# Causal attention in one kernel: the products that only serve the row maxima run as pairs of 64-row matmuls, the result gets a second bank, and the rotary sum moves to VectorE

## The chip, the core and the metric

The kernel runs on one core of a Trainium2 chip. Its engines are TensorE (PE in the rows, with its weight loads as PEld), VectorE (DVE), ScalarE (ACT), GpSimd (POOL) and SyncE (SP), which issues the transfers. The metric is the device time of one execution in microseconds (us). TensorE's results land in PSUM, which has eight banks of 512 fp32 columns; GpSimd has no access to PSUM.

## The reference

One transformer layer over 2048 tokens of width 512: a layer norm, attention with 32 query heads in 8 groups (4 query heads share one key head and one value head, all of width 64), and a feed-forward part with ternary weights. What matters here is the attention of one group:

```python
y = x * rsqrt(mean(x * x) + eps) * rms_w
q, k, v = split(y @ w_in.T)              # per group: 4 heads of q, one k, one v, width 64
q, k = rope(q), rope(k)                  # [x1*cos - x2*sin, x2*cos + x1*sin]
qk = (q @ k.T) * 64 ** -0.5              # causal: key <= query
attn = softmax(where(causal, qk, -inf))
o = attn @ v
```

## The kernel before

Everything fp32 is carried as two fp16 numbers, a high and a low part. After the norm (`normalise`), the function `attention` runs the eight groups one after another; then follow the output projection and the feed-forward part, which the change leaves alone.

In a group there are 16 **units** (4 chunks of 512 queries by 4 heads, `u = 4c + h`), and a unit of chunk c has 4(c+1) **steps**, one for each tile of 128 keys: 160 steps in a group. A step i goes through the engines so:

- `scores(i)` on TensorE: keys by queries, two products of 128 rows (high parts against `k_hl`, the low parts and the row maximum through `q_lm` and `k_h1`), and on the diagonal a third that adds the mask. The step is 512 columns wide, on the diagonal 512, 384, 256 and 128.
- `exps(i)` on ScalarE (L670) writes p in fp32; `low_part(i)` on GpSimd (L817) makes its low part.
- `values(i)` on TensorE, 5 steps later (`PV_LAG`): for each of up to four query tiles three matmuls of 64 or 65 columns (L619, L621, L623), which add up in the result bank `obank`.
- After the last step of a unit, `unit_out` on VectorE divides by the row sums (L776, L778); then ScalarE and GpSimd split the result in two parts (`unit_high`, `unit_low`).

The softmax needs each query's maximum **before** its scores are used. It comes from **pieces**: `max_piece` (L587) multiplies one tile of 128 queries with up to 512 keys, and VectorE reduces the bank (`reduce_piece`, L740, and L744 on the diagonal). There are 160 pieces in a group as well. The stationary tile is `q_hh`, which holds the high part of q twice, on rows 0 to 63 and on rows 64 to 127; `k_hl` holds the key's low part on rows 0 to 63 and its high part on rows 64 to 127, and `k_h1` holds the high part on rows 0 to 63. So a piece is (high q)(low k + high k). Any number near the true maximum serves, since it cancels out in the softmax.

Beside that, TensorE projects the coming tiles of 128 tokens (`project`, 12 matmuls of 384 columns, 16 tiles in a group). VectorE takes each out of its bank (`out_of_bank`): L763 and L769 for v, L765 and L766 for the products with cos and sin. GpSimd adds these (`rope_sum`, L823), and ScalarE and GpSimd split the sum (`qk_high_part`, `qk_low_part`).

The order on each engine is written out by hand: `SLOTS` has one slot for each step, with the projection and the pieces that ride in it. The pieces of a chunk are spread over a range of slots (`PIECE_SLOTS`), one or two in a slot. In a slot TensorE issues scores, the first piece, values, the projection, further pieces; where a unit begins, values come last. Pieces and projections share the **side banks** in turn (`take_bank`): with `SIDE = 4` an item waits until the reader of the item four places before it is done. The banks are 3 for scores, 4 at the side, and 1 for the result.

## Time and profile before

| | |
|---|---|
| median of 3 runs | 2151.24 us (2150.31 to 2152.04) |
| time of the profiled execution | 2150.29 us |
| its span, first to last instruction | 2148.2 us |
| attention, first to last step on GpSimd | 106.2 to about 1588 us |
| one group of eight (group 3) | 186.4 us, from 672.4 to 858.8 us |
| busy in that group: PE / POOL / DVE / ACT | 175.7 / 176.3 / 124.2 / 102.4 us |

Busy times are unions of an engine's instructions in a window. Matmuls are pipelined: a 512-column matmul is shown with 0.38 us, and the next starts 0.22 us after it. So the distance of the starts tells how much of TensorE a matmul takes, and a busy time of PE is a little too long at each place where it stops.

### The profile page before, as it was taken

The numbers are of one execution on the slowest core, as the hardware profiler recorded it, in microseconds if no ns is written. First come the engines' busy times: TensorE is split into PE (matmuls) and PEld (weight loads), VectorE is DVE, ScalarE is ACT, GpSimd is POOL, SyncE is SP. The second block draws the span as 40 slices with busy tenths as digits, with TensorE's granted clock in tenths as the row PEclk, the third lists the DMA queues.
The fourth block names the chain that finished last, engine by engine and source line by source line (L and its number), as shares of the span: only waits on it lengthen the run. The fifth ranks groups of instructions, "written<-read, shape, count | busy, mean of one in ns | idle before, by whom it ended". The sixth has DMA issues, their size and how long they took to land. (4 is left out here: it accounts for less than half of the span.)

```text
span 2148.2 us, 55361 instructions
## 1 busy us (share of the span) xinstructions
PE 1948.1 (91%) x21382; PEld 1178.0 (55%) x21382; DVE 1249.7 (58%) x3158; ACT 931.8 (43%) x1985; POOL 1587.4 (74%) x1803
## 2 busy tenths in 40 slices
PE   2599999999999999999999999999969988999998
PEld 1256666666666666666666666666634443444443
DVE  8567657757765764776576477657724772221221
ACT  3245555555555555555555555555541111111110
POOL 5489999999999999999999999999952441221311
PEclk7699999999999999999999999999989999999999
DMA  5432133124223312322332232223136530000000
GB/s 178 124 70 51 41 71 67 43 44 82 48 41 71 75 38 54 71 46 46 69 72 41 51 70 46 46 56 74 36 103 213 196 124 14 5 15 20 0 20 20
DMA packets 301573, 137.05 MB, mean 64 GB/s; under 512 B 248208, under 2 KB 285328, under 8 KB 299792
## 3 DMA queue, kind: packets, MB, share of 16 engines
q1 hardware_dynamic: 301328, 133.69, 26.4%
q8 instruction: 166, 2.72, 0.5%
q14 instruction: 79, 0.65, 0.1%
HBM read 49.74 MB, written 25.17 MB: 35 GB/s over the span
## 5 line engine op out<-in xcount | busy, mean ns | idle before, releaser
L817 POOL TENSOR_TENSOR pl<-p 128x512 f16<-128x512 f32 (+3 forms) x1280 | 1140.7, 919 | 89.0 <-ACT p L670 88.0
L670 ACT ACTIVATE p<-a_ps 128x512 f32<-128x512 f32 (+3 forms) x1280 | 676.3, 532 | 671.2 <-PE a_ps L603 430.5
L740 DVE TENSOR_REDUCE mpart<-a_ps 128x1 f32<-128x512 f32 x768 | 518.7, 687 | 169.4 <-PE a_ps L587 162.7
L619 PE MATMUL a_ps<-v,p 128*128 128x65 f16 x4352 | 528.5, 193 | 83.7 <-DVE onorm L778 60.7
L619 PEld LDWEIGHTS a_ps<-v,p 128*128 128x128 bf16 x4352 | 410.6, 97 | 218.9 <-DVE onorm L778 97.8
L621 PE MATMUL a_ps<-v,p 128*128 128x64 f16 x4352 | 530.1, 194 | 0.0
L623 PE MATMUL a_ps<-v,pl 128*128 128x65 f16 x4352 | 526.9, 192 | 0.0
L621 PEld LDWEIGHTS a_ps<-v,p 128*128 128x128 bf16 x4352 | 405.9, 97 | 98.4
L587 PE MATMUL a_ps<-k_hl,q_hh 128*128 128x512 f16 (+3 forms) x1280 | 439.8, 349 | 18.9 <-issue 11.4
L603 PE MATMUL a_ps<-q_lm,k_h 128*128 128x512 f16 (+3 forms) x1280 | 444.8, 347 | 0.0
L602 PE MATMUL a_ps<-q_hh,k_hl 128*128 128x512 f16 (+3 forms) x1280 | 444.1, 347 | 0.0
L623 PEld LDWEIGHTS a_ps<-v,pl 128*128 128x128 f16 x4352 | 407.2, 99 | 0.0
L744 DVE CUSTOM_DVE_ANT_0 masked<-a_ps,causal 128x128 bf16<-128x128 f32 (+3 forms) x512 | 247.9, 485 | 114.9 <-PE a_ps L587 107.9
L1264 POOL TENSOR_TENSOR f_hl<-f_hid,f_hh 128x512 f16<-128x512 f32 x64 | 74.2, 1161 | 239.9 <-DVE f_hh L1234 239.9
L1179 PE MATMUL f_ps<-xh,tern 128*128 (+1 forms) x512 | 195.0, 381 | 1.8 <-DVE f_credit L1221 1.8
L587 PEld LDWEIGHTS a_ps<-k_hl,q_hh 128*128 128x128 f16 x1280 | 124.0, 98 | 132.0 <-issue 14.0
L1179 PE MATMUL f_ps<-xl,tern 128*128 (+1 forms) x512 | 194.9, 381 | 0.0
L574 PE MATMUL a_ps<-wh,yh 128*128 128x384 f16 x512 | 168.8, 330 | 7.9 <-DVE wl L730 7.9
L984 PE MATMUL p_ps<-p_wh,p_att 128*128 128x512 f16 x512 | 158.6, 386 | 15.1 <-DMA p_att<-attn_scratch 15.1
L574 PE MATMUL a_ps<-wl,yh 128*128 128x384 f16 x512 | 168.8, 330 | 0.0
L574 PE MATMUL a_ps<-wh,yl 128*128 128x384 f16 x512 | 168.6, 329 | 0.0
L1215 ACT ACTIVATE f_silu<-f_ps,tern_scale 128x512 f32<-128x512 f32 x64 | 44.0, 687 | 256.7 <-PE f_ps L1179 256.7
(97 smaller groups left out, 2432.9 us busy)
## 6 DMA issues: line engine op xcount, KB each, us to landing
attn_scratch<-o_turn SPq DMA_DIRECT2D x64, 256.0 KB, 2.8
p_att<-attn_scratch SPq DMA_DIRECT2D x32, 512.0 KB, 4.5
raw<-ffn_t SPq DMA_DIRECT2D x12, 1024.0 KB, 5.0
wraw<-w_in_t SPq DMA_DIRECT2D x8, 768.0 KB, 5.2
resid_scratch<-xin SPq DMA_DIRECT2D x4, 1024.0 KB, 4.3
raw<-w_out_t SPq DMA_DIRECT2D x1, 4096.0 KB, 14.6
x<-resid_scratch SPq DMA_DIRECT2D x4, 1024.0 KB, 8.0
out<-x SPq DMA_DIRECT2D x16, 256.0 KB, 2.0
```

The lines of the kernel that those rows point to most:

```text
L574: last = nc.tensor.matmul(bank[:, 0:GC], a[:, kt, tok], b[:, kt, :], start=(kt == 0 and n == 0), stop=(kt == KT - 1 and n == 2))
L587: nc.tensor.matmul(bank[:, 0:width], q_hh[:, c % 2, h, t * P:(t + 1) * P], k_hl[:, par ^ ahead, kk * CHUNK:kk * CHUNK + width], start=True ...
L602: nc.tensor.matmul(out, k_hl[:, side, keys], q_hh[:, c % 2, h, r * P:CHUNK], start=True, stop=False)
L603: last = nc.tensor.matmul(out, k_h1[:, side, keys], q_lm[:, c % 2, h, r * P:CHUNK], start=False, stop=not diag)
L619: nc.tensor.matmul(o, weights, v[:, par, j, 0:VU], start=(j == 0 and t == 0), stop=False, skip_group_check=True)
L621: nc.tensor.matmul(o[:, 0:DH], weights, v[:, par, j, VL:VW], start=False, stop=False, skip_group_check=True)
L623: last = nc.tensor.matmul(o, pl[:, i % RING, t * P:(t + 1) * P], v[:, par, j, 0:VU], start=False, stop=(j == TPC * c + t), skip_group_chec ...
L670: nc.scalar.activation(p32[:, i % RING, r * P:CHUNK], sbank(i)[:, r * P:CHUNK], ACT.Exp, scale=SCALE).then_inc(exp_done, 1)
L740: nc.vector.reduce_max(mpart[:, u % 2, t, kk:kk + 1], bank, AX.X).then_inc(maxs_used, 1)
L744: nc.vector.tensor_tensor_reduce(masked[:, n % 2, 0:width], bank, causal[:, CHUNK - width:CHUNK], 1.0, -LEAST, ALU.add, ALU.max, mpart[:, ...
L817: nc.gpsimd.tensor_tensor(pl[:, i % RING, cols], p32[:, i % RING, cols], p_high[:, i % RING, cols], ALU.subtract).then_inc(low_ready, 1)
L1179: last = nc.tensor.matmul(bank, w[:, k, e * P:(e + 1) * P], x[:, k, bass.ds(c * CHUNK, CHUNK)], start=(k == 0 and x is xh), stop=(k == KT ...
```

## The change

Three things change in `attention`.

- **Pieces in pairs.** Two pieces that follow each other are issued together (`max_pair`). The first reads rows 0 to 63 of `q_hh` and of `k_h1`, the second rows 64 to 127 of `q_hh` and of `k_hl`; each contracts 64 rows and is (high q)(high k) alone. They go to two side banks. The slots are the same, but a slot has two pieces or none, and all pieces stand ahead of the slot's values and projection. The opening is arranged the same way.
- **Two result banks.** `OBANKS = 2`, so that the values of a unit wait for the unit before the last one to leave. For this `SIDE` goes from 4 to 3. `unit_out`, `unit_high` and `unit_low` come one step later.
- **The rotary sum on VectorE.** `out_of_bank` writes the sin product to a small `rope_b` (2 tiles instead of 4), the cos product back to its place in the bank, and the sum of the two to `rope_a`. GpSimd's `rope_sum` is gone. A side bank with a projection is now free after the sum (`roped_ready`), where it was free after L769 (`v_low`).

```diff
-SIDE = 4
-HIGH_LAG = PV_LAG + 1
-LOW_OUT_LAG = PV_LAG + 2
+SIDE = 3
+OBANKS = 2
+HIGH_LAG = PV_LAG + 2
+LOW_OUT_LAG = PV_LAG + 3
...
-        for n, piece in enumerate(chunk):
-            pieces[begin + n * (end - begin) // len(chunk)].append(piece)
+        for n in range(0, len(chunk), 2):
+            pieces[begin + n * (end - begin) // len(chunk)] += chunk[n:n + 2]
...
-        rope_b = sb("rope_b", [P, TILES_KEPT, HG + 1, DH], F32)
+        rope_b = sb("rope_b", [P, 2, HG + 1, DH], F32)
...
-        obank = ps[:, SBANKS + SIDE, 0:TPC * VU]
+        obank = lambda u: ps[:, SBANKS + SIDE + u % OBANKS, 0:TPC * VU]
...
-                        pe.wait_ge(v_low, (g + ahead) * TT + arg[0] + 1)
+                        pe.wait_ge(roped_ready, (g + ahead) * TT + arg[0] + 1)
...
-                def max_piece(ahead, u, i):
+                def max_pair(pair):
+                    ahead, u, i = pair[0]
                     c, h = divmod(u, HG)
-                    t, kk = divmod(i, c + 1)
...
-                    bank = take_bank("piece", ahead, u, i)
-                    width = CHUNK if kk < c else (t + 1) * P
-                    nc.tensor.matmul(bank[:, 0:width], q_hh[:, c % 2, h, t * P:(t + 1) * P],
-                                     k_hl[:, par ^ ahead, kk * CHUNK:kk * CHUNK + width], start=True, stop=True)\
-                        .then_inc(maxs_ready, 1)
+                    banks = [take_bank("piece", *piece) for piece in pair]
+                    for (_, _, i), bank, keys, rows in zip(pair, banks, (k_h1, k_hl), (slice(0, DH), slice(DH, P))):
+                        t, kk = divmod(i, c + 1)
+                        width = CHUNK if kk < c else (t + 1) * P
+                        nc.tensor.matmul(bank[:, 0:width], q_hh[rows, c % 2, h, t * P:(t + 1) * P],
+                                         keys[rows, par ^ ahead, kk * CHUNK:kk * CHUNK + width], start=True, stop=True)\
+                            .then_inc(maxs_ready, 1)
...
-                    if j == 0 and g + u:
-                        pe.wait_ge(o_out, g * UNITS + u)
+                    if j == 0 and g * UNITS + u >= OBANKS:
+                        pe.wait_ge(o_out, g * UNITS + u + 1 - OBANKS)
...
-                    for piece in pieces[:1]:
-                        max_piece(*piece)
+                    for n in range(0, len(pieces), 2):
+                        max_pair(pieces[n:n + 2])
...
-                    dve.wait_ge(qk_low, gg * TT + t + 1)
                     nc.vector.tensor_scalar(v[:, side, t, 0:DH], bank[:, ROPED:GC], 1.0 / W_SCALE, None,
                                             ALU.mult).then_inc(v_high, 1)
-                    nc.vector.tensor_tensor(roped(rope_a), halves, by_half(cos[:, t, :]), ALU.mult)
-                    nc.vector.tensor_tensor(roped(rope_b), halves[:, :, ::-1, :], by_half(sin[:, t, :]), ALU.mult)\
+                    if gg * TT + t >= 2:
+                        dve.wait_ge(roped_ready, gg * TT + t - 1)
+                    nc.vector.tensor_tensor(by_head(rope_b[:, t % 2]), halves[:, :, ::-1, :], by_half(sin[:, t, :]), ALU.mult)\
                         .then_inc(rope_parts, 1)
+                    dve.wait_ge(rope_parts, 2 * (gg * TT + t) + 1)
+                    nc.vector.tensor_tensor(halves, halves, by_half(cos[:, t, :]), ALU.mult).then_inc(rope_parts, 1)
                     dve.wait_ge(v_high, gg * TT + t + 1)
                     nc.vector.scalar_tensor_tensor(v[:, side, t, VL:VW], bank[:, ROPED:GC], 1.0 / W_SCALE,
-                                                   v[:, side, t, 0:DH], ALU.mult, ALU.subtract).then_inc(v_low, 1)
+                                                   v[:, side, t, 0:DH], ALU.mult, ALU.subtract)
+                    dve.wait_ge(rope_parts, 2 * (gg * TT + t) + 2)
+                    dve.wait_ge(qk_low, gg * TT + t + 1)
+                    nc.vector.tensor_tensor(by_head(rope_a[:, b]), halves, by_head(rope_b[:, t % 2]), ALU.add)\
+                        .then_inc(roped_ready, 1)
...
-                    if step is not None and step - PV_LAG + 1 in FIRST_STEP[1:]:
-                        unit_out(FIRST_STEP.index(step - PV_LAG + 1) - 1)
+                    if step is not None and step - PV_LAG in FIRST_STEP[1:]:
+                        unit_out(FIRST_STEP.index(step - PV_LAG) - 1)
...
-                def rope_sum(ahead, t):
-                    b = t % TILES_KEPT
-                    pool.wait_ge(rope_parts, (g + ahead) * TT + t + 1)
-                    nc.gpsimd.tensor_tensor(rope_a[:, b], rope_a[:, b], rope_b[:, b], ALU.add).then_inc(roped_ready, 1)
```

On TensorE, at slots 9 to 11 of the first group (unit 1 begins in its values), before the change. L602 and L603 are scores, L587 pieces, L619, L621 and L623 values; names in brackets are the semaphores waited for.

```order
L602 MATMUL a_ps<-q_hh,k_hl 128x512 [waits exp_done]
L603 MATMUL a_ps<-q_lm,k_h 128x512
L587 MATMUL a_ps<-k_hl,q_hh 128x128 [waits maxs_used]
L619 MATMUL a_ps<-v,p 128x65 [waits low_ready,exp_done,o_out]
...
L602 MATMUL a_ps<-q_hh,k_hl 128x512 [waits exp_done]
L603 MATMUL a_ps<-q_lm,k_h 128x512
L587 MATMUL a_ps<-k_hl,q_hh 128x512 [waits maxs_used]
L619 MATMUL a_ps<-v,p 128x65 [waits low_ready,exp_done]
...
L602 MATMUL a_ps<-q_hh,k_hl 128x512 [waits exp_done]
L603 MATMUL a_ps<-q_lm,k_h 128x512
L587 MATMUL a_ps<-k_hl,q_hh 128x256 [waits maxs_used]
L619 MATMUL a_ps<-v,p 128x65 [waits low_ready,exp_done]
```

The same place after it; L603 and L604 are scores now, L588 the pieces, L620, L622 and L624 values.

```order
L603 MATMUL a_ps<-q_hh,k_hl 128x512 [waits exp_done]
L604 MATMUL a_ps<-q_lm,k_h 128x512
L620 MATMUL a_ps<-v,p 128x65 [waits low_ready,exp_done,o_out]
...
L603 MATMUL a_ps<-q_hh,k_hl 128x512 [waits exp_done]
L604 MATMUL a_ps<-q_lm,k_h 128x512
L588 MATMUL a_ps<-k_h,q_hh 128x512 [waits maxs_used]
L588 MATMUL a_ps<-k_hl,q_hh 128x256
L620 MATMUL a_ps<-v,p 128x65 [waits low_ready,exp_done]
...
L603 MATMUL a_ps<-q_hh,k_hl 128x512 [waits exp_done]
L604 MATMUL a_ps<-q_lm,k_h 128x512
L620 MATMUL a_ps<-v,p 128x65 [waits low_ready,exp_done]
```

The piece of slot 9 has gone to slot 8, that of slot 11 to slot 10, and the two of slot 10 read `k_h` and `k_hl`; between a pair and the next stand products of 128 rows. The first values of the unit still name `o_out`, but with a smaller value.

On VectorE, where unit 0 leaves its bank and a tile is taken out in the same slot, before:

```order
L776 RECIPROCAL rden<-a_ps 128x4 [waits pv_done]
L778 TENSOR_TENSOR onorm<-a_ps,rden 128x256 [waits o_rden]
L763 TENSOR_SCALAR v<-a_ps 128x64 [waits qk_low,misc_ready]
L765 TENSOR_TENSOR rope_a<-a_ps,cos_sb 128x320
L766 TENSOR_TENSOR rope_b<-a_ps,sin_sb 128x320
L769 SCALAR_TENSOR_TENSOR v<-a_ps,v 128x64 [waits v_high]
L744 ISA masked,mpart<-a_ps,causal 128x128 [waits maxs_used,maxs_ready]
```

The same after:

```order
L761 TENSOR_SCALAR v<-a_ps 128x64 [waits misc_ready]
L765 TENSOR_TENSOR rope_b<-a_ps,sin_sb 128x320 [waits roped_ready]
L768 TENSOR_TENSOR a_ps<-a_ps,cos_sb 128x320 [waits rope_parts]
L770 SCALAR_TENSOR_TENSOR v<-a_ps,v 128x64 [waits v_high]
L774 TENSOR_TENSOR rope_a<-a_ps,rope_b 128x320 [waits qk_low,rope_parts]
L781 RECIPROCAL rden<-a_ps 128x4 [waits pv_done]
L783 TENSOR_TENSOR onorm<-a_ps,rden 128x256 [waits o_rden]
```

The tile's part has a fifth instruction, the sum, and a wait between the two products; the unit's part (L776 and L778 before, L781 and L783 after) has moved behind the tile's, one slot later.

On GpSimd, in the same stretch (L817 low parts of p, L823 the rotary sum, L832 low parts of q and key, L840 the low part of a result), before:

```order
L840 TENSOR_TENSOR o_hl<-onorm,o_hl 128x4x64 [waits o_high]
L817 TENSOR_TENSOR pl<-p 128x512 [waits exp_done] x2
L823 TENSOR_TENSOR rope_a<-rope_a,rope_b 128x320 [waits rope_parts]
L832 TENSOR_TENSOR qk_lo<-rope_a,qk_hi 128x5x64 [waits qk_high]
L817 TENSOR_TENSOR pl<-p 128x512 [waits exp_done] x2
L840 TENSOR_TENSOR o_hl<-onorm,o_hl 128x4x64 [waits o_high]
```

And after (L820, L830, L838):

```order
L838 TENSOR_TENSOR o_hl<-onorm,o_hl 128x4x64 [waits o_high]
L820 TENSOR_TENSOR pl<-p 128x512 [waits exp_done]
L830 TENSOR_TENSOR qk_lo<-rope_a,qk_hi 128x5x64 [waits qk_high]
L820 TENSOR_TENSOR pl<-p 128x512 [waits exp_done] x3
L838 TENSOR_TENSOR o_hl<-onorm,o_hl 128x4x64 [waits o_high]
```

The sum is gone from the queue, and the result's low part comes one step later.

## Rows read from the trace of the kernel before

**Rows 1.** The page: its first line and its row of PE.

```profile
span 2148.2 us, 55361 instructions
...
PE 1948.1 (91%) x21382; PEld 1178.0 (55%) x21382; DVE 1249.7 (58%) x3158; ACT 931.8 (43%) x1985; POOL 1587.4 (74%) x1803
```

**Rows 2.** Busy time by stage of group 3, stages cut at L817 starts.

```profile
core 0: us, PE busy (x) PEld busy (x) DVE busy (x) ACT busy (x) POOL busy (x), PEclk, DMA share, GB/s
672.40:691.40 19.00, 18.92 (x210) 12.61 (x207) 14.77 (x48) 10.21 (x28) 16.76 (x25) 1.00 0.36 78
691.40:709.00 17.60, 16.20 (x244) 10.98 (x243) 13.08 (x38) 11.07 (x24) 17.59 (x23) 1.00 0.35 69
709.00:728.90 19.90, 18.85 (x226) 12.13 (x225) 13.70 (x40) 9.09 (x23) 18.79 (x25) 1.00 0.24 54
728.90:755.80 26.90, 25.66 (x364) 17.02 (x363) 22.99 (x56) 16.80 (x37) 26.32 (x30) 1.00 0.39 71
755.80:783.90 28.10, 25.74 (x354) 16.93 (x352) 18.70 (x45) 14.74 (x32) 25.86 (x31) 1.00 0.10 21
783.90:807.90 24.00, 22.82 (x291) 14.27 (x287) 16.66 (x42) 13.47 (x28) 22.54 (x27) 1.00 0.36 67
807.90:823.20 15.30, 14.83 (x226) 9.96 (x226) 11.02 (x26) 9.14 (x17) 15.30 (x19) 1.00 0.14 29
823.20:846.50 23.30, 23.13 (x306) 15.50 (x307) 10.29 (x41) 12.88 (x33) 20.91 (x25) 1.00 0.15 30
846.50:858.80 12.30, 9.57 (x174) 6.71 (x171) 2.95 (x12) 5.02 (x10) 12.17 (x15) 1.00 0.64 130
sum 186.40, PE 175.71 PEld 116.11 DVE 124.15 ACT 102.41 POOL 176.26; mean PE 19.52 PEld 12.90 DVE 13.79 ACT 11.38 POOL 19.58
```

**Rows 3.** Line L817 (POOL): count, and first and last start.

```profile
L817 POOL TENSOR_TENSOR pl<-p x1280: 389/1038/1362, 106.2 to 1587.6; 128x512 f16<-128x512 f32 x130, 128x256 f16<-128x256 f32 x19, 128x128 f16<-128x128 f32 x17, 128x384 f16<-128x384 f32 x17
```

**Rows 4.** Waits in group 3: engine, line, awaited: us in total, times, longest.

```profile
PEld a_ps L619 <- DVE onorm L778: 12.4, 11, 2.1
POOL pl L817 <- ACT p L670: 10.0, 13, 1.4
PE a_ps L619 <- DVE onorm L778: 7.7, 10, 1.8
```

**Rows 5.** Timeline around 700 us: start us, us, instruction [idle before it].

```profile
699.88 0.38 PE L603 MATMUL a_ps<-q_lm,k_h 128*128 128x512 f16 x1
...
700.10 0.38 PE L587 MATMUL a_ps<-k_hl,q_hh 128*128 128x512 f16 x1
...
700.32 0.19 PE L619 MATMUL a_ps<-v,p 128*128 128x65 f16 x1
...
702.49 0.33 PE L587 MATMUL a_ps<-k_hl,q_hh 128*128 128x384 f16 x1
...
703.51 0.10 PEld L619 LDWEIGHTS a_ps<-v,p 128*128 128x128 bf16 x1 [0.98 <-DVE onorm L778]
703.51 0.20 PE L619 MATMUL a_ps<-v,p 128*128 128x65 f16 x1 [0.70 <-DVE onorm L778]
```

**Rows 6.** Timeline of POOL, one sum of the rotation.

```profile
713.03 0.87 POOL L823 TENSOR_TENSOR rope_a<-rope_a,rope_b 128x320 f32<-128x320 f32 x1
713.85 1.84 POOL L817 TENSOR_TENSOR pl<-p 128x512 f16<-128x512 f32 x2
```

**Rows 7.** Timeline of DVE: a projected tile, then a unit out.

```profile
676.65 0.22 DVE L763 TENSOR_SCALAR v<-a_ps 128x64 f16<-128x64 f32 x1 [0.68 <-PE a_ps L574]
676.79 0.48 DVE L765 TENSOR_TENSOR rope_a<-a_ps,cos_sb 128x320 f32<-128x320 f32 x1
677.19 0.48 DVE L766 TENSOR_TENSOR rope_b<-a_ps,sin_sb 128x320 f32<-128x320 f32 x1
677.59 0.21 DVE L769 SCALAR_TENSOR_TENSOR v<-a_ps,v 128x64 f16<-128x64 f32 x1
677.72 0.55 DVE L744 CUSTOM_DVE_ANT_0 masked<-a_ps,causal 128x384 bf16<-128x384 f32 x1
...
680.20 0.17 DVE L776 RECIPROCAL rden<-a_ps 128x4 f32<-128x4 f32 x1
680.41 0.42 DVE L778 TENSOR_TENSOR onorm<-a_ps,rden 128x256 f32<-128x256 f32 x1
```

More of the change, by code:

```diff
@@ L307, in side_work @@
 def side_work(part):
-    return [item for _, job, pieces in part
-            for item in [("piece", *p) for p in pieces[:1]] + ([job] if job else []) + [("piece", *p) for p in pieces[1:]]]
+    return [item for _, job, pieces in part for item in [("piece", *p) for p in pieces] + ([job] if job else [])]
 OPENING_SIDE = side_work(OPENING)
@@ L637, in group @@
                         project(*job[1:])
-                    for piece in pieces[1:]:
-                        max_piece(*piece)
                     if starts_unit:
```

19 lines of the change are left out of this document (7 added, 12 removed).

## The prediction

> **What bounds the kernel now.** The span is 2148.2 us and the execution took 2150.3, 0.9 under the median of 2151.2 [rows 1]. I read first where attention lies: its 1280 steps start on GpSimd between 106.2 and 1587.6 us, so it has 1481 us of the span, or 7.9 times the 186.4 us of group 3 [rows 2, 3]. The rest isn't touched.
>
> Then the windows of group 3, in nine stages cut at the start of L817 in steps 0, 16, 32, 48, 72, 96, 116, 132 and 148 [rows 2]. Two engines are nearly full, and they take turns. PE is the fuller one in the first stage (18.9 of 19.0 us) and in 823 to 846 (23.1 of 23.3), where four projections lie in each. POOL is it in 691 to 709 (17.6 of 17.6), 729 to 756 (26.3 of 26.9), 808 to 823 and the last stage (12.2 of 12.3, PE 9.6). Elsewhere they are equal within 0.3 us. The clock is at 1.00 in all stages, the 2.4 GHz level. If each stage took just its fuller engine's time, the group would take
>
> 18.9 + 17.6 + 18.9 + 26.3 + 25.9 + 22.8 + 15.3 + 23.1 + 12.2 = 181.0 us.
>
> It takes 5.4 us more. The waits say why: at the first values of a unit TensorE waits for the result bank, 12.4 us seen from the weight load and 7.7 seen from the matmul, in 10 or 11 of 16 units; and POOL waits 10.0 us in all for ScalarE, which had its scores late from TensorE [rows 4]. The timeline shows one: a piece of 384 columns starts at 702.49, and the next matmul at 703.51 [rows 5].
>
> **Part 1, the pairs.** A 512-column matmul follows the one before by 0.22 us [rows 5], 1/2.4 GHz a column. If the two of a pair run side by side, a pair costs its wider half. The pieces go in the order of a unit, so the pairs of chunk 0 are (128, 256) and (384, 512): 256 columns or 0.107 us saved a pair on average. For chunk 1 it is (512, diagonal), 320 columns or 0.133 us; for chunk 2, 384 columns or 0.160; for chunk 3, 416 columns or 0.173. That is 12.4 us a group for 80 pairs, if nothing is paid.
>
> What is paid is unknown. Each pair stands between products of 128 rows, so TensorE changes from 128 to 64 rows and back for each, 160 times a group, and no matmul of the trace has 64 rows. From below the price is 0: nothing says that a change costs, and where the kind of product changes now, the next starts after 0.22 us as among equals [rows 5]. From above it is all that a matmul lasts beyond its columns, 0.38 − 0.22 = 0.16 us (I calculate with 0.165), as if each change let the pipe run empty. A weight load should not come on top: after the stop at 703.51 load and matmul start together [rows 5]. I take 0.05 us a change, nearer to the row that shows no loss, since a next matmul can be under way while the last one ends, as all do here. Then a pair gains 0.007, 0.033, 0.060 or 0.073 us by chunk.
>
> A rule speaks against the change. The Trainium skill (TensorEngine Tiling (Array Packing), Key Properties) says that changing the tiling mode drains TensorE, and gives no time. By it the price would be towards the upper bound, and the sum ends at the slower rival below. No run here shows it.
>
> **Part 2, the rotary sum leaves POOL.** One takes 0.82 us of the queue (713.03 to 713.85) [rows 6]; 16 a group are 13.1 us. By the slots of the projections they lie 3, 1, 3, 1, 2, 2, 0, 4, 0 in the nine stages. On DVE the products with cos and sin follow each other by 0.40 us [rows 7]; the sum is of the same size, with one operand in PSUM as they have, so 0.40 us more. The cos product now waits for the sin product: as L778 behind L776, which starts 0.21 us after a start of 0.17 us length [rows 7], a wait costs about 0.04 plus the 0.08 of overlap lost, 0.12 us. So a tile is 0.5 to 0.65 us longer, 10 us a group. DVE has 124 of 186 us. Its fullest stage (729 to 756) goes from 23.0 to 23.6 of 25.5, the first from 14.8 to about 17 of 18.6 us: hidden. If it weren't, each tile would cost its 0.6.
>
> **Part 3, two result banks, three side banks.** The first values of a unit no longer wait for its predecessor. The wait that follows is for the unit before that, 8 steps or more back: gone. I leave 2 us of the 5.4 for other waits: the low part and the exponential are still awaited at some values, and the pieces now want two of three banks at once. A pair needs the bank of the projection three items back; VectorE holds it now 1.14 + 0.6 = 1.7 us (676.65 to 677.79 before) [rows 7], then must reduce the first piece of the pair between. That is some 2.5 us, and TensorE has 2 to 3 slots of work, 2.2 to 3.4 us, before it asks. So nearly free; the price if not is 0.5 us at each of 16 projections.
>
> **The sum.** By stage, PE less its pairs' gain (8, 8, 9.6, 14.4, 12.8, 10.7, 8.5, 4.6, 3.4 pairs by the slots), POOL less its sums:
>
> | stage | PE | POOL | fuller |
> |---|---|---|---|
> | 0 to 16 | 18.6 | 14.3 | 18.6 |
> | 16 to 32 | 15.9 | 16.8 | 16.8 |
> | 32 to 48 | 18.4 | 16.3 | 18.4 |
> | 48 to 72 | 24.8 | 25.5 | 25.5 |
> | 72 to 96 | 24.8 | 24.2 | 24.8 |
> | 96 to 116 | 22.0 | 20.9 | 22.0 |
> | 116 to 132 | 14.2 | 15.3 | 15.3 |
> | 132 to 148 | 23.1 | 17.6 | 23.1 |
> | 148 to 160 | 9.6 | 12.2 | 12.2 |
>
> Together 176.7, with 2 us of waits 178.7, against 186.4: 7.7 us a group, times 7.9 is 61 us. 2151.2 − 61 = 2090 us. Of this the waits give 3.4 us a group, the sums about 2, the pairs about 2.
>
> **Rivals.**
>
> - *Side by side, and a change costs nothing.* PE's stages come to 17.8, 15.1, 17.4, 23.4, 23.5, 20.9, 13.3, 22.6, 9.2; with POOL's the fuller ones are 172.7, with 2 us 174.7. The gain is 11.7 × 7.9 = 92 us: 2058 us. For it speaks that all kinds of products follow each other without a gap; against it, that POOL then leads in four stages, and its own waits would show. The Trainium skill (TensorE: Matmul & The Clock Gate, the part on packing small matmuls) has matmuls on different rows start about 4 ns apart; by it the pairs do run side by side, and no row here can say.
> - *A change costs the whole pipe, 0.165 us.* A pair then loses 0.223, 0.197, 0.170 or 0.157 us by chunk, PE leads in all stages but the last (20.5, 17.8, 20.5, 28.1, 27.7, 24.5, 16.1, 24.1, and POOL's 12.2), 191.5 us, with 2 us 193.5. That is 7.1 × 7.9 = 56 us slower: 2207 us. The two sums cross 186.4 at about 0.11 us a change, from which it decides. For it speaks the 0.16 us in the rows and the rule above; against it, that nothing but a full stop of the pipe would cost so much, and that weights are loaded ahead everywhere else.
> - *The two halves run one after the other, and a change is free.* PE keeps its 175.7; only the sums and the bank help: fuller ones 179.4, with 2 us 181.4, 5.0 × 7.9 = 40 us gained: 2111 us. At 0.05 us a change it is close to no change.
> - *Side banks too few.* 0.5 us at each of 16 projections, 8 us a group, eats the gain of the main case: about 2150 us. For it speaks that VectorE's queue is in order and the projection's five instructions come ahead of the next pieces; against it, the 2.2 to 3.4 us that TensorE has.
>
> **How the numbers follow.** Side by side at a price near 0.05 us (0.02 to 0.10): 0.45, with 2072 to 2135 us. Free change: 0.14. One after the other: 0.10, half of it with a gain that counts. A price over 0.11 us: 0.22. Side banks: 0.09, about evenly on both sides of no change. What a measurement can tell here is about 0.2%, 4.3 us. Faster by more: 0.45 + 0.14 + 0.08 + 0.04 = 0.71. Within: 0.05. Slower: 0.24. The likeliest case's own range is 2072 to 2135; the range for 8 in 10 has to reach over the free change down to 2055 and up to the costly one, 2200.
>
> **What would show it.** In the profile after: the two starts of a pair within some hundredths of a us (side by side) or 0.22 us apart (in turn); the time from the second start of a pair to the first values, 0.22 us plus a change, and the same ahead of the pair; no wait of L620 for the result; POOL without 13 us a group, with more waits for ScalarE in the first stage; DVE near 134 us a group; waits of the pieces for `roped_ready` (VectorE's sum) near none. The forecast is wrong if the distance around a pair is 0.11 us or more over its columns, or if the pieces wait for VectorE by over 0.3 us at each projection, or if POOL's queue turns out slower where VectorE is busier.

## The result and the profile after

The changed kernel takes 2167.4 us (median of 4 runs, 2166.4 to 2167.9), and the kernel before 2151.6 us (4 runs, 2150.3 to 2154.3). The ratio is 1.0071, with a 95% interval of 1.0054 to 1.0088. The change makes the kernel 15.7 us slower, where the forecast was 61 us faster. The profiled execution took 2167.9 us.

First the page, as in [rows 1]:

```profile
span 2165.9 us, 55913 instructions
...
PE 1979.5 (91%) x21382; PEld 1094.0 (51%) x21382; DVE 1284.5 (59%) x3286; ACT 928.8 (43%) x1985; POOL 1491.8 (69%) x1675
```

The line of the 1280 steps on GpSimd, as in [rows 3]:

```profile
L820 POOL TENSOR_TENSOR pl<-p x1280: 394/1038/1357, 109.4 to 1604.3; 128x512 f16<-128x512 f32 x130, 128x256 f16<-128x256 f32 x19, 128x128 f16<-128x128 f32 x17, 128x384 f16<-128x384 f32 x17
```

Attention starts 3.2 us later and ends 16.7 us later. It takes 1494.9 us, 13.5 more, and what follows it takes 561.6 us as against 560.6. So the loss is in the groups and a little in the opening. GpSimd has 96 us less to do and the kernel is still slower. TensorE, whose pairs should have saved it time, is busy 31 us longer.

The stages of group 3, cut at the same steps as in [rows 2]:

```profile
682.50:702.20 19.70, 17.52 (x195) 10.48 (x191) 15.05 (x46) 9.73 (x26) 13.90 (x21) 1.00 0.26 47
702.20:720.70 18.50, 18.26 (x248) 10.58 (x246) 14.17 (x43) 10.78 (x26) 16.83 (x23) 1.00 0.54 99
720.70:740.90 20.20, 18.79 (x221) 10.79 (x219) 14.23 (x41) 9.52 (x23) 16.47 (x22) 1.00 0.32 56
740.90:768.70 27.80, 26.27 (x363) 14.89 (x364) 23.40 (x57) 16.41 (x36) 26.25 (x30) 1.00 0.34 68
768.70:797.20 28.50, 28.09 (x377) 16.33 (x375) 20.37 (x50) 15.46 (x33) 24.49 (x30) 1.00 0.10 21
797.20:820.20 23.00, 22.54 (x290) 12.52 (x288) 16.14 (x40) 12.86 (x27) 21.07 (x24) 1.00 0.35 70
820.20:835.50 15.30, 15.30 (x235) 8.96 (x232) 10.85 (x29) 8.86 (x18) 15.30 (x18) 1.00 0.10 20
835.50:858.10 22.60, 22.60 (x286) 14.04 (x283) 11.88 (x46) 12.79 (x31) 17.94 (x22) 1.00 0.31 37
858.10:870.40 12.30, 10.05 (x179) 6.87 (x178) 2.42 (x10) 5.67 (x13) 12.15 (x16) 1.00 0.45 102
sum 187.90, PE 179.42 PEld 105.47 DVE 128.51 ACT 102.08 POOL 164.41; mean PE 19.94 PEld 11.72 DVE 14.28 ACT 11.34 POOL 18.27
```

The group takes 187.9 us, where it took 186.4. POOL has 11.9 us less, and in the first three stages it is not full (13.9 of 19.7, 16.8 of 18.5 and 16.5 of 20.2 us). TensorE fills the second of them (18.3 of 18.5 us), but is busy 17.5 of 19.7 us in the first and 18.8 of 20.2 in the third. Neither engine bounds those two; something both wait for does. The clock is at 1.00 throughout this group, the 2.4 GHz level, as before. The waits of the group, as in [rows 4]:

```profile
POOL pl L820 <- ACT p L669: 23.0, 35, 1.8
...
PEld a_ps L588 <- issue: 17.4, 46, 1.0
PEld a_ps L620 <- issue: 16.9, 71, 0.6
PEld a_ps L588 <- DVE mpart L739: 10.3, 21, 1.4
...
PE a_ps L588 <- DVE mpart L739: 5.3, 10, 1.1
PEld a_ps L588 <- DVE rope_a L774: 3.7, 4, 1.5
```

The wait of the values for the result bank is gone. In its place the pieces (L588) wait for VectorE, for its reductions (L739) and for its rotary sum (L774). POOL waits for ScalarE 23.0 us, not 10.0: it has lost work and gained idle time. The two "issue" rows are stops without any awaited engine. The timeline shows what they are:

```profile
712.14 0.38 PE L603 MATMUL a_ps<-q_hh,k_hl 128*128 128x512 f16 x1
712.14 0.10 PEld L604 LDWEIGHTS a_ps<-q_lm,k_h 128*128 128x128 f16 x1
...
712.35 0.38 PE L604 MATMUL a_ps<-q_lm,k_h 128*128 128x512 f16 x1
...
712.66 0.09 PEld L588 LDWEIGHTS a_ps<-k_h,q_hh 64*128 64x128 f16 x1 [0.42 <-issue]
712.66 0.09 PEld L588 LDWEIGHTS a_ps<-k_hl,q_hh 64*128 64x128 f16 x1
712.66 0.39 PE L588 MATMUL a_ps<-k_h,q_hh 64*128 64x512 f16 x1
712.67 0.28 PE L588 MATMUL a_ps<-k_hl,q_hh 64*128 64x256 f16 x1
...
712.98 0.10 PEld L620 LDWEIGHTS a_ps<-v,p 128*128 128x128 bf16 x1 [0.22 <-issue]
712.98 0.20 PE L620 MATMUL a_ps<-v,p 128*128 128x65 f16 x1
```

The two matmuls of the pair start 0.01 us apart: they do run side by side. But L603 is followed by L604 after 0.21 us, and L604 by the pair after 0.31 us, and the pair by the values after 0.32 us, though its wider half has the same 512 columns. That is the price of a change. Read from the finer starts of the trace, it is 0.310 − 0.2155 = 0.095 us on the way to 64 rows, and 0.318 − 0.2155 = 0.103 us on the way back. The second matmul of a pair starts 0.003 to 0.006 us after the first. So a pair pays 0.198 us and saves 0.107 to 0.173 us: 80 pairs pay 15.8 us a group and save 12.4. A little more is lost behind a pair: the first six short matmuls of the values take 0.012 us more together than in full_rows below, where the pieces have 128 rows. That is up to 1.0 us a group more, or 8 us over attention.

The rows also show what differs at a change: elsewhere a weight load starts a matmul ahead of its own (L604's with L603's matmul), and here it starts with it. The load lasts 0.09 to 0.10 us, about the price. Whether the pipe's running out or the load holds the start back, no run separates.

And the timeline of VectorE, a projected tile with the two reductions behind it, for comparison with [rows 7]; one row of PE is left in it, the first piece that is reduced here:

```profile
704.39 0.23 DVE L761 TENSOR_SCALAR v<-a_ps 128x64 f16<-128x64 f32 x1 [1.22 <-PE a_ps L573]
704.53 0.48 DVE L765 TENSOR_TENSOR rope_b<-a_ps,sin_sb 128x320 f32<-128x320 f32 x1
705.05 0.50 DVE L768 TENSOR_TENSOR a_ps<-a_ps,cos_sb 128x320 f32<-128x320 f32 x1
705.46 0.21 DVE L770 SCALAR_TENSOR_TENSOR v<-a_ps,v 128x64 f16<-128x64 f32 x1
...
705.52 0.39 PE L588 MATMUL a_ps<-k_h,q_hh 64*128 64x512 f16 x1
...
705.59 0.48 DVE L774 TENSOR_TENSOR rope_a<-a_ps,rope_b 128x320 f32<-128x320 f32 x1
705.99 0.17 DVE L781 RECIPROCAL rden<-a_ps 128x4 f32<-128x4 f32 x1
706.20 0.42 DVE L783 TENSOR_TENSOR onorm<-a_ps,rden 128x256 f32<-128x256 f32 x1
706.54 0.68 DVE L739 TENSOR_REDUCE mpart<-a_ps 128x1 f32<-128x512 f32 x1
707.14 0.42 DVE L743 CUSTOM_DVE_ANT_0 masked<-a_ps,causal 128x256 bf16<-128x256 f32 x1
```

The tile holds its bank from 704.39 to 706.07 us, 1.68 us instead of 1.14. Then follows a unit's result, and then come both pieces of a pair. These were issued at 705.52 us and keep two of the three side banks until 707.2 and 707.6. VectorE stood idle 1.22 us just ahead of all this. It is 59% busy on the whole, and late in such places.

### The profile page after: what moved, and what is told of

Read it like the earlier page. It is cut to its first block and busy times, and to the rows that moved or that the text cites. A ratio compares the mean times of both kernels' runs of the same rounds, so it can differ in the third digit from the quotient of the medians.

```text
span 2165.9 us, 55913 instructions
## 1 busy us (share of the span) xinstructions
PE 1979.5 (91%) x21382; PEld 1094.0 (51%) x21382; DVE 1284.5 (59%) x3286; ACT 928.8 (43%) x1985; POOL 1491.8 (69%) x1675
## 5 line engine op out<-in xcount | busy, mean ns | idle before, releaser
L820 POOL TENSOR_TENSOR pl<-p 128x512 f16<-128x512 f32 (+3 forms) x1280 | 1144.5, 919 | 190.8 <-ACT p L669 186.5
L739 DVE TENSOR_REDUCE mpart<-a_ps 128x1 f32<-128x512 f32 x768 | 509.3, 686 | 173.2 <-PE a_ps L588 171.9
L620 PE MATMUL a_ps<-v,p 128*128 128x65 f16 x4352 | 535.0, 194 | 20.4 <-POOL pl L820 15.7
L622 PE MATMUL a_ps<-v,p 128*128 128x64 f16 x4352 | 531.0, 194 | 0.0
L624 PE MATMUL a_ps<-v,pl 128*128 128x65 f16 x4352 | 527.4, 192 | 0.0
L620 PEld LDWEIGHTS a_ps<-v,p 128*128 128x128 bf16 x4352 | 402.5, 97 | 222.7 <-issue 135.9
L604 PE MATMUL a_ps<-q_lm,k_h 128*128 128x512 f16 (+3 forms) x1280 | 444.9, 348 | 0.0
L603 PE MATMUL a_ps<-q_hh,k_hl 128*128 128x512 f16 (+3 forms) x1280 | 443.7, 347 | 0.0
L622 PEld LDWEIGHTS a_ps<-v,p 128*128 128x128 bf16 x4352 | 407.3, 98 | 42.1
L624 PEld LDWEIGHTS a_ps<-v,pl 128*128 128x128 f16 x4352 | 407.9, 99 | 0.0
L588 PE MATMUL a_ps<-k_h,q_hh 64*128 64x512 f16 (+2 forms) x640 | 232.0, 363 | 64.9 <-DVE mpart L739 40.7
L743 DVE CUSTOM_DVE_ANT_0 masked<-a_ps,causal 128x128 bf16<-128x128 f32 (+3 forms) x512 | 242.2, 482 | 46.7 <-PE a_ps L588 46.1
L588 PE MATMUL a_ps<-k_hl,q_hh 64*128 64x512 f16 (+3 forms) x640 | 220.4, 344 | 0.0
L588 PEld LDWEIGHTS a_ps<-k_h,q_hh 64*128 64x128 f16 x640 | 59.2, 93 | 286.8 <-issue 145.4
```

The lines of the kernel that those rows point to most:

```text
L588: nc.tensor.matmul(bank[:, 0:width], q_hh[rows, c % 2, h, t * P:(t + 1) * P], keys[rows, par ^ ahead, kk * CHUNK:kk * CHUNK + width], star ...
L603: nc.tensor.matmul(out, k_hl[:, side, keys], q_hh[:, c % 2, h, r * P:CHUNK], start=True, stop=False)
L604: last = nc.tensor.matmul(out, k_h1[:, side, keys], q_lm[:, c % 2, h, r * P:CHUNK], start=False, stop=not diag)
L620: nc.tensor.matmul(o, weights, v[:, par, j, 0:VU], start=(j == 0 and t == 0), stop=False, skip_group_check=True)
L622: nc.tensor.matmul(o[:, 0:DH], weights, v[:, par, j, VL:VW], start=False, stop=False, skip_group_check=True)
L624: last = nc.tensor.matmul(o, pl[:, i % RING, t * P:(t + 1) * P], v[:, par, j, 0:VU], start=False, stop=(j == TPC * c + t), skip_group_chec ...
```

## The experiments

All are measured against the kernel before on the same chip. Its medians there were 2152.1 us (for full_rows, single64, banks and rope), 2152.4 (banks_rope, banks_full, banks_pairs and pairs), 2150.9 (banks_split, banks_rope_sb and banks_lag6) and 2152.1 (side3). Each difference in us is against that median.

### One part undone, one part alone

**full_rows**: the changed kernel, but both pieces of a pair are products of 128 rows on `k_hl`, as before (they include the key's low part again). Order, banks and the rotary sum stay as changed.

```diff
-for (_, _, i), bank, keys, rows in zip(pair, banks, (k_h1, k_hl), (slice(0, DH), slice(DH, P))):
+for (_, _, i), bank, keys, rows in zip(pair, banks, (k_hl, k_hl), (slice(0, P), slice(0, P))):
```

> The changed kernel with the two pieces of a pair as 128-row products again (both on k_hl), all else as changed. Theory one (changing between 128 and 64 rows costs TensorE about 0.10 us each way): 160 changes, 16 us a group, go, and 12.4 us of columns come back, so some 3 to 4 us a group less than the changed kernel's 187.8: about 2140 us, and below the kernel before. Theory two (the pieces wait for VectorE's side banks, the changes themselves cost little): the waits stay and the columns come back, 2200 us or more.

Measured: 2161.7 us, 1.0038 (1.0025 to 1.0051). The pairs cost only 6 us on top of a kernel that is already 9.6 us slower without them. So the price of the change is not the whole cause, nor the larger part of it: order, banks and sum, where I saw a gain of 40 us (the rival "halves in turn", 2111 us), lose 10. Of the 77 us between forecast and result, 50 are in these parts, and 27 in the pairs' rows (21 us forecast as a gain, 6 measured as a loss). The time lies between the two that were expected.

**single64**: the kernel before, with each piece a product of 64 rows. It leaves out the key's low part in the maximum's product.

```diff
-nc.tensor.matmul(bank[:, 0:width], q_hh[:, c % 2, h, t * P:(t + 1) * P],
-                 k_hl[:, par ^ ahead, kk * CHUNK:kk * CHUNK + width], start=True, stop=True)\
+nc.tensor.matmul(bank[:, 0:width], q_hh[0:DH, c % 2, h, t * P:(t + 1) * P],
+                 k_h1[0:DH, par ^ ahead, kk * CHUNK:kk * CHUNK + width], start=True, stop=True)\
```

> The kernel before with each single piece as a 64-row product (rows 0 to 63 of q_hh and k_h1), nothing else changed. Theory one: 320 changes a group at 0.10 us are 32 us of TensorE, of which some 10 fill its present stops: 20 us a group or more, 2290 to 2400 us. Theory two: the same time as before, 2151 us, since no bank, order or other engine changes.

Measured: 2372.3 us, 1.1008 (1.0990 to 1.1027), 220 us slower for the same columns. Its timeline:

```profile
700.77 0.38 PE L603 MATMUL a_ps<-q_lm,k_h 128*128 128x512 f16 x1
...
701.09 0.39 PE L587 MATMUL a_ps<-k_h,q_hh 64*128 64x512 f16 x1
...
701.40 0.20 PE L619 MATMUL a_ps<-v,p 128*128 128x65 f16 x1
```

The distances around the piece are 0.32 and 0.31 us, with nothing beside it. It pays both changes alone, twice as often as the pairs: 160 × 0.198 = 31.7 us a group, of which 26 to 29 us are seen (213.6 to 215.1 us for groups 1 to 6). The price belongs to the change of rows and not to the pair.

**banks**: before, with two result banks, three side banks and the later `unit_out`, and nothing else.

```diff
-SIDE = 4
-HIGH_LAG = PV_LAG + 1
-LOW_OUT_LAG = PV_LAG + 2
+SIDE = 3
+OBANKS = 2
+HIGH_LAG = PV_LAG + 2
+LOW_OUT_LAG = PV_LAG + 3
...
-                    if j == 0 and g + u:
-                        pe.wait_ge(o_out, g * UNITS + u)
+                    if j == 0 and g * UNITS + u >= OBANKS:
+                        pe.wait_ge(o_out, g * UNITS + u + 1 - OBANKS)
```

> The kernel before with two result banks and three side banks alone (with the later steps for the unit's way out). Theory one: the stops at the first values of a unit go, 181 us of the fuller engines and 2 to 3 us of other waits a group: about 2125 us. Theory two: three side banks make the pieces wait for VectorE, no gain or a loss, 2150 us or more.

Measured: 2112.3 us, 0.9806 (0.9790 to 0.9822): 39.8 us faster, 13 us under the time expected, and the fastest kernel of the study. The last row of the same nine windows, for its group 3:

```profile
sum 181.40, PE 175.50 PEld 116.53 DVE 123.81 ACT 102.19 POOL 176.07; mean PE 19.50 PEld 12.95 DVE 13.76 ACT 11.35 POOL 19.56
```

The sum of the fuller engine by stage was 181.0 us; here the group takes 181.4. The change of banks was worth 5.0 us in group 3 (4.4 in group 4, which takes 182.0), where I had counted 3.4. By their own stages the fuller engines of this kernel come to 179.7 us, so that 1.7 us of other waits are left. The run has the later `unit_out` as well; no run has the second bank without it.

**rope**: before, with the rotary sum on VectorE alone (four side banks, one result bank).

```diff
-                        pe.wait_ge(v_low, (g + ahead) * TT + arg[0] + 1)
+                        pe.wait_ge(roped_ready, (g + ahead) * TT + arg[0] + 1)
...
+                    nc.vector.tensor_tensor(by_head(rope_a[:, b]), halves, by_head(rope_b[:, t % 2]), ALU.add)\
+                        .then_inc(roped_ready, 1)
...
-                    nc.gpsimd.tensor_tensor(rope_a[:, b], rope_a[:, b], rope_b[:, b], ALU.add).then_inc(roped_ready, 1)
```

> The kernel before with the rotary sum on VectorE alone, four side banks, one result bank. POOL loses 13 us a group, but leads in three stages only: 1 to 2 us a group, about 2140 us. By theory two a projection's bank is held longer and VectorE is later with the pieces and with the unit's result, so that it is 2150 us or more.

Measured: 2185.7 us, 1.0144 (1.0127 to 1.0161): 33.6 us slower. The waits over attention (130 to 1590 us), of the kernel before and then of this one:

```profile
PE a_ps L619 <- DVE onorm L778: 60.7, 81, 1.8
```

```profile
PE a_ps L617 <- DVE onorm L782: 79.3, 79, 2.3
```

The result leaves its one bank through the same queue as the tiles. A tile that takes 0.54 us longer makes the result later, and the values wait for it, 18.6 us more. The clock accounts for most of the other 15 us. In the kernel before it stays at 1.00 from 130 us to the end of attention. Here it falls eleven times for a short stretch to 0.5, the 1.2 GHz level, behind 11 of its 14 stops of 2.2 or 2.3 us at the first values of a unit. One of them, from the timeline of TensorE and from the windows (us, then busy times, and the clock third from the end):

```profile
379.48 0.20 PE L617 MATMUL a_ps<-v,p 128*128 128x65 f16 x1 [2.18 <-DVE onorm L782]
```

```profile
379.80:383.00 3.20, 3.20 (x27) 1.75 (x25) 1.53 (x4) 1.50 (x4) 1.41 (x2) 0.50 0.51 118
```

Groups 1, 3 and 5 have two such stretches and take 191.9 us, and groups 2, 4 and 6 have one and take 190.4. So one costs 1.5 us, and eleven some 16.

### The parts together

These four build up to the changed kernel and break off at each part.

**banks_rope**: banks and rope, with the pieces in their old places.

```diff
+OBANKS = 2
...
+                        pe.wait_ge(roped_ready, (g + ahead) * TT + arg[0] + 1)
```

> Two result banks, three side banks and the rotary sum on VectorE, with single 128-row pieces in their old slots (no pairs). Alone, the sum on VectorE cost 34 us, mostly as a later result bank; with two result banks that wait is gone. If that was all, the sum is free or gains a little of POOL's 13 us: 2100 to 2112 us, beside 2112 for the banks alone. If the sum makes VectorE late for three side banks, the pieces wait as in the changed kernel (its trace has 10 us a group ahead of pieces beyond the changes of rows): 2135 to 2165 us.

**banks_full**: banks, with pieces in pairs in every second slot, ahead of values and projection, as products of 128 rows; the sum on GpSimd.

```diff
+        for n in range(0, len(chunk), 2):
+            pieces[begin + n * (end - begin) // len(chunk)] += chunk[n:n + 2]
...
+                    for n in range(0, len(pieces), 2):
+                        max_pair(pieces[n:n + 2])
...
+for (_, _, i), bank, keys, rows in zip(pair, banks, (k_hl, k_hl), (slice(0, P), slice(0, P))):
```

> Two result banks, three side banks, pieces two in a slot but as 128-row products, the rotary sum on GpSimd. It differs from the banks alone by the arrangement of the pieces. If asking for two of three side banks at once is what makes the pieces wait, 3 us a group or more stay: 2135 to 2160 us. If the rotary sum on VectorE was behind those waits: 2112 to 2120 us.

**banks_pairs**: the same with products of 64 rows, the halves of the change.

```diff
-for (_, _, i), bank, keys, rows in zip(pair, banks, (k_hl, k_hl), (slice(0, P), slice(0, P))):
+for (_, _, i), bank, keys, rows in zip(pair, banks, (k_h1, k_hl), (slice(0, DH), slice(DH, P))):
```

> Two result banks, three side banks, pairs of 64-row products, the rotary sum on GpSimd. Beside the same with 128-row products it saves 12.4 us of columns a group and pays 80 times 0.198 us, 15.8 us, read from the starts of the changed kernel: 3.4 us a group more at most, 0 to 27 us over that kernel. If the changes were hidden by other waits, the two are equal.

**pairs**: before, with the pairs of 64 rows alone (four side banks, one result bank, the sum on GpSimd).

```diff
-        for n, piece in enumerate(chunk):
-            pieces[begin + n * (end - begin) // len(chunk)].append(piece)
+        for n in range(0, len(chunk), 2):
+            pieces[begin + n * (end - begin) // len(chunk)] += chunk[n:n + 2]
...
-                    for piece in pieces[:1]:
-                        max_piece(*piece)
+                    for n in range(0, len(pieces), 2):
+                        max_pair(pieces[n:n + 2])
...
+                    for (_, _, i), bank, keys, rows in zip(pair, banks, (k_h1, k_hl), (slice(0, DH), slice(DH, P))):
```

> The kernel before with pairs of 64-row products alone: four side banks, one result bank, sum on GpSimd. By the price of the changes, 3.4 us a group more: about 2175 us. With four side banks the pieces should not wait for VectorE. A rival: the pair stands ahead of all values and delays the first values' turn less than single pieces did, so that the wait for the result bank grows as well: 2190 us or more.

Measured, with the first ones (the last column is group 4 in us, read from the starts on GpSimd; 1 + 4 is one result bank and four side banks):

| kernel | pieces | banks | sum on | median | ratio (95%) | us | group 4 |
|---|---|---|---|---|---|---|---|
| before | single | 1 + 4 | GpSimd | 2151.6 | | 0 | 186.4 |
| banks | single | 2 + 3 | GpSimd | 2112.3 | 0.9806 (0.9790 to 0.9822) | −39.8 | 182.0 |
| banks_rope | single | 2 + 3 | VectorE | 2127.1 | 0.9886 (0.9867 to 0.9906) | −25.3 | 183.1 |
| banks_full | two, 128 rows | 2 + 3 | GpSimd | 2137.1 | 0.9930 (0.9910 to 0.9949) | −15.3 | 184.1 |
| banks_pairs | two, 64 rows | 2 + 3 | GpSimd | 2159.8 | 1.0037 (1.0023 to 1.0051) | +7.4 | 187.9 |
| full_rows | two, 128 rows | 2 + 3 | VectorE | 2161.7 | 1.0038 (1.0025 to 1.0051) | +9.6 | 187.7 |
| changed | two, 64 rows | 2 + 3 | VectorE | 2167.4 | 1.0071 (1.0054 to 1.0088) | +15.7 | 187.8 |
| rope | single | 1 + 4 | VectorE | 2185.7 | 1.0144 (1.0127 to 1.0161) | +33.6 | 190.4 |
| pairs | two, 64 rows | 1 + 4 | GpSimd | 2194.8 | 1.0195 (1.0175 to 1.0215) | +42.4 | 191.5 |

Counted from banks: the sum on VectorE costs 14.5 us, two pieces in one slot 24.5, and both together 49.4, so 10 more than the two apart. The 64 rows in place of 128 cost 22.7 us without the sum (banks_full to banks_pairs), but 6.1 with it (full_rows to changed). banks_rope lies between its two expectations, banks_full and banks_pairs within one of theirs.

pairs came out as its rival had it (2190 us or more). Its wait for the result grew from 60.7 to 70.6 us, seen from the matmul as in rope, and the clock fell to the 1.2 GHz level six times between 130 us and the end of attention; its groups without such a stretch take 191.5 us, 5.1 more than before, where the price less the columns is 3.4 and the loss behind the pairs 1.0. With four side banks the pieces hardly stop TensorE for VectorE, though they come two in a slot: 2.3 us in all, seen from the matmul, where the changed kernel has 39.9 us for L739 alone.

The starts on TensorE explain much of this last difference. In group 4, I added up by how much the pieces (and the second of two, where it starts apart from the first) start later than the columns before them account for. The change back is 80 × 0.103. All in us:

| | ahead of the pairs | change back | columns saved | together |
|---|---|---|---|---|
| banks_full | 5.7 | 0 | 0 | 5.7 |
| banks_pairs | 12.5 | 8.2 | −12.4 | 8.3 |
| full_rows | 9.6 | 0 | 0 | 9.6 |
| changed | 15.0 | 8.2 | −12.4 | 10.8 |

With the sum on GpSimd, 64 rows add 6.8 us ahead of the pairs, nearly the full 80 × 0.095 = 7.6, and 2.6 us net. With it on VectorE the pairs wait longer for a bank anyway. They add 5.4 us, and 1.2 net: where TensorE stands for VectorE, the change is paid while it stands. The starts show it: behind a stop of over 0.25 us, a pair starts 0.135 us after VectorE's release in the changed kernel, and 0.136 us in full_rows, where no rows change. Times eight groups the net is 21 and 10 us, against 22.7 and 6.1 measured, and what is lost behind the pairs comes on top of both. Group 4 itself grows by 3.8 and by 0.1 us, so the sums over the pieces do not hold for every group. Part of the rest is the clock: from 130 us to the end of attention the traced execution of banks_full has two short stretches at the 1.2 GHz level, banks_pairs five, full_rows three and the changed kernel one, nearly all at the end of a group, where one costs about 1 us by the groups of banks_pairs (186.7 us without, 187.3 to 188.0 with).

The waits over attention (130 to 1590 us) of banks, banks_rope and banks_full, in this order:

```profile
PEld a_ps L588 <- DVE v L770: 19.2, 23, 1.2
...
PEld a_ps L588 <- DVE mpart L741: 10.5, 14, 0.9
```

```profile
PEld a_ps L586 <- DVE rope_a L774: 34.2, 38, 1.7
...
PEld a_ps L586 <- DVE mpart L739: 15.2, 30, 0.9
```

```profile
PEld a_ps L590 <- DVE mpart L741: 44.9, 93, 1.5
...
PEld a_ps L590 <- DVE v L770: 8.0, 8, 1.0
```

With the sum on VectorE the pieces wait for the tile's bank, 34.2 us where it was 19.2. With two pieces in one slot they wait for each other's banks, 93 times where it was 14.

### Why two pieces in one slot cost

**banks_split**: banks, with two pieces in every second slot, but not back to back. The first stands ahead of the values, the second behind them, both with 128 rows.

```diff
-        for n, piece in enumerate(chunk):
-            pieces[begin + n * (end - begin) // len(chunk)].append(piece)
+        for n in range(0, len(chunk), 2):
+            pieces[begin + n * (end - begin) // len(chunk)] += chunk[n:n + 2]
```

> The two result banks, with two pieces in every second slot as in the changed kernel, but as 128-row products of which the first stands ahead of the slot's values and the second behind them (and the opening as before). If the 25 us of the arrangement come from taking two of three side banks back to back, they go: about 2112 us. If they come from two pieces reaching VectorE in one slot, they stay: 2130 to 2140 us.

Measured: 2136.8 us, 0.9932 (0.9918 to 0.9947), which is banks_full's time within its interval. So it isn't that TensorE asks for two banks at the same moment. What both kernels have, and banks has not, is two pieces in one slot and none in the next. They bring VectorE its work in bursts, and that costs about 25 us with three side banks, wherever in the slot they stand. The pieces' longest wait is now for the tile's bank:

```profile
PE a_ps L588 <- DVE v L770: 24.5, 38, 1.4
```

In banks this row has 4.5 us and 8 times.

**side3**: before with three side banks and nothing else.

```diff
-SIDE = 4
+SIDE = 3
```

> The kernel before with three side banks instead of four, one bank unused, nothing else. If the fourth side bank was worth something to single pieces, TensorE waits for VectorE ahead of pieces (3 us a group, as with the two result banks): 2155 to 2175 us, and the second result bank by itself is then worth more than the 40 us measured. If single pieces never need it: 2151 us.

Measured: 2163.2 us, 1.0049 (1.0032 to 1.0066): 11.1 us slower. A wait has come that the kernel before doesn't have:

```profile
PEld a_ps L587 <- DVE v L769: 19.3, 23, 1.2
```

It is the same row as in banks (19.2, 23 times). The fourth side bank was worth 11 us, and the second result bank with its later `unit_out`, given three side banks, 39.8 + 11.1 = 51 us.

### Two attempts at a better version

**banks_rope_sb**: banks with the sum on VectorE, but both products in SBUF as before, so that the side bank is free after L770 and the sum reads no bank.

```diff
+                    nc.vector.tensor_tensor(rope_a[:, b], rope_a[:, b], rope_b[:, b], ALU.add).then_inc(roped_ready, 1)
...
-                    nc.gpsimd.tensor_tensor(rope_a[:, b], rope_a[:, b], rope_b[:, b], ALU.add).then_inc(roped_ready, 1)
```

> The two result banks and the rotary sum on VectorE, but with both products in SBUF and the side bank free after the fourth instruction as before; the sum comes fifth, out of SBUF. If the 15 us of the sum come from the longer hold of the bank, most of them go: 2105 to 2115 us. If they come from VectorE's added time of 0.4 to 0.5 us a tile, they stay: about 2127 us. If a VectorE sum with both operands in SBUF is held up beside GpSimd's work, it lasts over 0.5 us and the time is above 2127.

Measured: 2164.3 us, 1.0061 (1.0047 to 1.0076): 39 us slower than banks_rope. The sum's line in the list of groups, here and then in the changed kernel (busy us, mean ns of one):

```profile
L774 DVE TENSOR_TENSOR rope_a<-rope_a,rope_b 128x320 f32<-128x320 f32 x128 | 147.5, 1152 | 0.0
```

```profile
L774 DVE TENSOR_TENSOR rope_a<-a_ps,rope_b 128x320 f32<-128x320 f32 x128 | 62.4, 487 | 0.0
```

The same sum takes 1152 ns with both operands in SBUF (492 at best, 3689 at worst) and 487 ns (484 to 490) with one in PSUM. The difference is GpSimd's: 109 of the 128 sums took over 0.6 us, and each of these began while a GpSimd instruction ran, and ended 0.34 to 0.35 us after the end of one. The Trainium skill (SBUF — State Buffer, SBUF: two separate sides) has a VectorE instruction with two SBUF inputs and a GpSimd instruction that reads SBUF shut each other out; the trace agrees. The question that the run was for stays open in part. The wait for the tile's bank went back to what banks has (19.3 us, where banks_rope has 34.2), but the longer sum brought more than that in other waits.

**banks_lag6**: banks with the values 6 steps behind the scores instead of 5, since its largest remaining wait is that of the values for p.

```diff
-PV_LAG = 5
+PV_LAG = 6
```

> The two result banks with values 6 steps behind scores instead of 5, ring of 10 as before. With the banks alone TensorE stops for 4 to 6 us a group at values that await the exponential or the low part; if those are local mismatches, a sixth step removes half of them: 2100 to 2108 us. If the ring then makes ScalarE wait for the values ten steps back, or the engines are full over their stages already (181.0 us of fuller engines against 181.4), it is 2112 us or more.

Measured: 2140.3 us (2135.0 to 2147.0), 0.9954 (0.9938 to 0.9970): 29 us slower than banks. The wait of the values went down (PEld of L620 for ScalarE from 39.6 us to 8.4). But a new one came, few and long:

```profile
PE a_ps L588 <- DVE mpart L745: 14.9, 4, 3.7
```

These are 14.9 of the 29 us. VectorE's timeline shows what starts them, and GpSimd's what runs beside it:

```profile
181.82 5.23 DVE L731 SCALAR_TENSOR_TENSOR wl<-wraw,wh 128x384 f16<-128x384 f32 x1
```

```profile
181.67 4.96 POOL L818 TENSOR_TENSOR pl<-p 128x256 f16<-128x256 f32 x6
```

It is the same effect as in banks_rope_sb. L731 makes a low part of the weights, with both operands in SBUF. Wherever it is prolonged, here, in banks and in the kernel before, it began beside a GpSimd instruction and ends 0.41 to 0.42 us after the end of one. It takes at most 1.3 us in banks, but 5.2 us four times here, while GpSimd makes low parts without a gap. The reduction behind it in the queue frees the bank late. Groups 1, 3 and 4, with such a stop, take 186.6 to 187.4 us, and groups 2, 5 and 6, without, 182.4 to 183.3. Behind each of the four stops the clock falls to the 1.2 GHz level, and five times more at the end of a group, where banks has one such stretch in all. Why GpSimd has this backlog with a sixth step, no run shows.

## Why the prediction was wrong

**The bound, right.** Two engines that take turns, with 5.4 us a group for the result bank between them: banks gives 181.4 us where the sum of the fuller engines was 181.0. The term for other waits, 2 us, was about right: banks keeps 1.7 us over its own fuller engines, which are themselves 1.3 us below those of before. That the group comes within 0.4 us of the old sum is in part luck.

**Part 1, the pairs: the mechanism right, the price wrong.** They run side by side. The step that failed is "I take 0.05 us a change". It measured 0.095 and 0.103, between my bounds of 0 and 0.165. My reason was that a next matmul is under way while the last one ends. For a change of rows it is so only in part: a time of 0.10 us, of the 0.16 that a matmul lasts beyond its columns, is lost each time. The Trainium skill (TensorEngine Tiling (Array Packing), Key Properties) has a change of tiling mode drain TensorE. The trace fits it, with 0.10 us seen at each end, but can't tell a drain from a weight load that is not taken ahead. I also named 0.11 us as the price from which the change loses, but that counted the other parts' gains. By their columns alone the pairs lose from 12.4 / 160 = 0.078 us on. With 0.198 us a pair where I took 0.10, TensorE has 7.8 us a group more, and my table's fuller engines come to 181.8 + 2 = 183.8 us: 20 us faster and not 61. So by my table the price alone takes 40 of the 77 us by which I missed; but the parts below take the whole gain without it, as full_rows shows.

**Part 2, the sum on VectorE: sizes right, "hidden" wrong.** POOL lost the sums (11.9 us of its busy time in group 3, for 13.1), a tile is 0.54 us longer (I had 0.5 to 0.65), and VectorE's busy time rose less than 10 us, from 124.2 to 128.5. The step that failed is to hide 0.6 us a tile under the idle time of a stage. VectorE's queue is in order, and behind the tile stand the reductions that free the banks and, with one result bank, the result. The sum costs 14.5 us with two result banks and 33.6 with one, of which some 16 by the clock that fell behind the longer stops. What it takes off POOL was worth little: its wait for ScalarE rose by 13.0 us in group 3, as much as it lost in sums.

**Part 3, the banks: one half right.** The wait for the result is gone, and the banks alone bring 40 us, not the 27 of my 3.4 × 7.9, although the lost side bank costs 11 by itself. "So nearly free" is the step that failed. I counted the time between a projection and the next pieces, 2.2 to 3.4 us of work against 2.5 of VectorE, as if those pieces were the only ones. Three side banks instead of four cost 11 us by themselves (side3). Two pieces in every second slot cost 24.5 us, and 35 when the tile is longer too (banks_rope to full_rows). I had priced this rival at 8 us a group and given it 0.09. Its size is about what happened: from banks to full_rows the group grows by 6 us. Its mechanism is half of it: in full_rows the weight loads of the pieces wait 30.2 us for a tile's bank over attention, as the rival had it, and 46.7 us for the bank of another full-width piece, which it had not. Without any change of rows the kernel would already be slower than before.

**The account.** Banks −40, the sum +14.5, two pieces in a slot +24.5, both together another +10, and 64 rows +6: 15.7 us. The 64 rows cost 23 where the sum is on GpSimd and VectorE is waited for less. **The chances.** I gave slower 0.24, nearly all of it for a price over 0.11 us. The price stayed under it, so that "slower" came true for another reason than I had given. Two slips stand in that part: of "one after the other", 0.10, I said that half gains, and then counted 0.08 as faster; and with a free change POOL leads in five stages, not four. Neither changes the forecast. What decides is two steps that I had each set at nearly nothing because VectorE has idle time.

## What to carry to other kernels

The share of idle time of an in-order engine does not say how late it is: ask what stands in its queue behind the work that you add, and which bank that frees, and spread the work it gets evenly over the slots. Halves of TensorE's rows run side by side, but a pair of them between full-row matmuls pays some 0.20 us for going there and back at the 2.4 GHz level, as much as 475 columns, so that even two full ones of 512 gain next to nothing. By these numbers many such pairs would have to follow each other; no run here has that. When a change has several parts, run the cheapest alone: here the result bank by itself, with `SIDE` 3, is the version to keep, at 2112.3 us, 1.9% under the kernel before.
